# A vision-transformer block on one core: the token-mixing network in five batches, row sums spread over the steps, loads reordered

## What is computed

```python
def _L0_tok_ref(x, w1, b1, w2, b2):
    w = x.sum(axis=1).mean(axis=2)
    h = jax.nn.gelu(w @ w1.T + b1)
    w = h @ w2.T + b2
    w = w.reshape(B, C, G).transpose(2, 0, 1)
    w = jax.nn.softmax(w, axis=0)
    out = jnp.einsum('bgcd,gbc->bcd', x, w)
    return out
...
h = _L0_tok_ref(x, w1, b1, w2, b2)
h = h + attention(layernorm(h))      # 16 heads of 16, causal, 128 tokens an image
h = h + mixture_of_experts(layernorm(h))   # 64 experts, 6 a token, and a shared one
```

## Time and profile before

| stretch, us | what runs | PE | DVE | ACT | POOL | PE clock |
|---|---|---|---|---|---|---|
| 0 to 30 | loads, batch 0 to 3, steps -2 | 8.10 | 14.74 | 7.01 | 4.26 | 1.00 |
| 30 to 75 | steps -1, 0, most of 1 | 33.19 | 17.19 | 27.16 | 2.95 | 0.66 |
| 75 to 240 | steady steps | 158.46 | 145.54 | 132.81 | 94.57 | 1.00 |
| 240 to 300 | loop's end, tables | 45.04 | 41.65 | 15.39 | 33.04 | 0.89 |
| 300 to 510 | expert tiles | 198.07 | 87.07 | 96.41 | 116.06 | 1.00 |
| 510 to 559 | rest of the shared expert, final sums | 29.18 | 33.89 | 2.39 | 1.97 | 0.78 |

### The profile page before, as it was taken

How to read it: one execution, slowest core, us unless ns; L and a number is a source line. 1 busy time by engine, 2 the same in 40 slices (tenths; PEclk the granted TensorE clock), 3 DMA queues, 4 the chain that set the end, 5 groups by cost and what they waited for, 6 DMA issues and landing times. The chain is left out here.

```text
span 559.0 us, 12585 instructions
## 1 busy us (share of the span) xinstructions
PE 472.0 (84%) x2990; PEld 355.2 (64%) x2991; DVE 340.1 (61%) x1054; ACT 281.2 (50%) x910; POOL 252.8 (45%) x277
## 2 busy tenths in 40 slices
PE   0466899999999999987679999999999999997923
PEld 0343676777776766654437787787787787783522
DVE  3715367998999999887753343443443444441797
ACT  2257478877788887871113444444454454441000
POOL 1100111466666666666741546555565565544000
PEclk9967689999999999997899999999999999998967
DMA  8999920011111111121234568557577746542996
GB/s 270 346 333 288 284 60 2 30 67 69 68 59 58 58 66 68 71 75 68 105 110 121 187 190 276 166 170 236 173 211 214 222 143 207 178 150 92 414 360 251
DMA packets 57589, 91.04 MB, mean 163 GB/s; under 512 B 7911, under 2 KB 44650, under 8 KB 57552
## 3 DMA queue, kind: packets, MB, share of 16 engines
q1 hardware_dynamic: 44880, 62.41, 36.9%
q0 software_dynamic: 10368, 26.07, 13.0%
q10 hardware_dynamic: 2304, 2.10, 1.1%
HBM read 87.09 MB, written 41.60 MB: 230 GB/s over the span
## 5 line engine op out<-in xcount | busy, mean ns | idle before, releaser
L392 POOL DMA_INDIRECT y_rows<-y,xring x120 | 118.0, 984 | 108.0 <-issue 67.1
L1021 PE MATMUL ps<-wring,prob 128*128 x480 | 124.5, 382 | 9.1 <-ACT prob L543 9.1
L970 DVE TENSOR_TENSOR probt<-probt,ps 128x128 f32<-128x128 f32 x120 | 34.5, 287 | 119.2 <-ACT probt L548 108.5
L1021 PEld LDWEIGHTS ps<-wring,prob 128*128 128x128 f32 x480 | 81.8, 190 | 17.6 <-issue 11.5
L450 ACT ACTIVATE prob<-ps,nmax 128x128 f32<-128x128 f32 x256 | 69.6, 388 | 5.1 <-DVE nmax L676 3.9
L1021 PE MATMUL ps<-wring,probt 128*128 x240 | 72.0, 382 | 0.0
L548 ACT ACTIVATE probt<-ps 128x128 f32<-128x128 f32 x120 | 33.3, 277 | 71.4 <-PE ps L1021 71.4
L543 ACT COPY prob<-ps 128x256 f32<-128x256 f32 x121 | 45.0, 373 | 47.4 <-PE ps L1236 44.8
L978 DVE TENSOR_SCALAR y<-ps,xring 128x256 f32<-128x256 f32 x120 | 57.8, 483 | 6.4 <-PE ps L1021 4.1
L365 POOL DMA_INDIRECT slot_rows<-row,slot_ix x48 | 52.7, 1097 | 13.7 <-issue 13.4
L365 POOL DMA_INDIRECT slot_rows<-xring,slot_ix x48 | 51.0, 1062 | 14.0 <-issue 14.0
(11 more groups left out here) (177 smaller groups left out, 779.6 us busy)
## 6 DMA issues: line engine op xcount, KB each, us to landing
wring<-wexp SPq DMA_DIRECT2D x121, 384.0 KB
xring<-slot_rows SPq DMA_DIRECT2D x121, 129.0 KB, 2.1
x_sb<-y_rows SPq DMA_DIRECT2D x16, 768.0 KB, 7.3
slot_rows<-pads SPq DMA_DIRECT2D x1, 8256.0 KB, 36.5
x_sb<-x SPq DMA_DIRECT2D x3, 2048.0 KB, 17.8
slot_rows<-pads SPq DMA_DIRECT2D x5, 516.0 KB, 10.3
x_sb<-x SPq DMA_DIRECT2D x4, 512.0 KB, 5.9
out<-h_all ACTq DMA_DIRECT2D x16, 128.0 KB, 6.9
```

The costliest lines, as they stand in the source:

```text
L392: nc.gpsimd.indirect_dma_start(out=y_dram, out_offset=bass.IndirectOffsetOnAxis(ap=xring[:, q, TO_AT:TO_AT + 1].bitcast(I32), axis=0), in_ ...
L970: nc.vector.tensor_tensor(hm[:, q % 2, :], silu[:, q % 2, :], psS[q % 2][:, INTER:2 * INTER], ALU.mult).then_inc(S("h_ready"), 1)
L1021: return nc.tensor.matmul(*a, **k)
```

## The change

The mixing network runs in five batches: image 0, images 1 to 3, then 4 to 7, 8 to 11 and 12 to 15. `part_at` gives each batch its PSUM bank and columns; batches 3 and 4 use columns 64 and up of psC, which the loop also uses. `weights` is split into `shift` and `weights`. Image 0 is mixed, normed and applied ahead of images 1 to 3, whose network runs between (`first_norm`, `first_apply`, and `mixing_in(1)`, `mixing_out(1)` around step -2's turn of image 0); the bias product (`bv_projected`) goes to the end of step -2. Batch 2 keeps the places of the former second batch, in steps 0 and 1. Batches 3 and 4 run in steps 3 and 4, and 7 and 8. ScalarE's row sums, formerly at the top of steps -2, -1 and 0 and inside step 0, stand one or two a step in steps -1 to 6, behind the exponentials of the step. VectorE's sums stand ahead of the loop (image 3) and in step -1 (images 6 and 7). w2 and b2 are loaded ahead of image 1, the constants ahead of image 2.

```diff
--- before.py
+++ after.py
@@ -247,9 +247,16 @@
-        PARTS = ((0, 4), (4, NB))
-        ACT_SUMS = {-3: (0, 2), -2: (4, 5), -1: (6, 7, 8), 0: (9, 10, 12, 14)}
-        DVE_SUMS = {-3: (1, 3), 0: (11, 13, 15)}
+        PARTS = ((0, 1), (1, 4), (4, 8), (8, 12), (12, NB))
+        PART_AT = {0: 2, 3: 3, 7: 4}
+        ACT_SUMS = {-3: (0, 1, 2), -1: (4, 5), 0: (8,), 1: (9,), 2: (10, 11), 3: (12,), 4: (13,), 5: (14,), 6: (15,)}
+        DVE_SUMS = {-3: (3,), -1: (6, 7)}
+        def part_at(part):
+            bank, col = ((psA, 0), (psX, 0), (psC, 0), (psC, E), (psC, E))[part]
+            n = PARTS[part][1] - PARTS[part][0]
+            return bank[0:HID, col:col + n], bank[:, col:col + NG * n]
         TABLES = 4
@@ -279,14 +286,18 @@
         def _(sp):
-            for j in range(4):
+            def load_image(j):
                 sp.dma_start(x_sb[:, j, :, :], x[j].rearrange("g c d -> c g d")).then_inc(x_in[j], 16)
-                if j == 0:
-                    sp.dma_start(w1_sb[:], w1t).then_inc(weights_in["w1"], 16)
-                    sp.dma_start(b1_sb[:], b1).then_inc(weights_in["b1"], 16)
+            load_image(0)
+            sp.dma_start(w1_sb[:], w1t).then_inc(weights_in["w1"], 16)
+            sp.dma_start(b1_sb[:], b1).then_inc(weights_in["b1"], 16)
             sp.dma_start(w2_sb[:], w2t).then_inc(weights_in["w2"], 16)
             sp.dma_start(b2_sb[:], b2).then_inc(weights_in["b2"], 16)
+            load_image(1)
             sp.dma_start(const_sb[:], const).then_inc(const_in, 16)
+            load_image(2)
+            load_image(3)
             sp.dma_start(wqkv_sb[:], wqkv).then_inc(weights_in["wqkv"], 16)
@@ -353,8 +364,9 @@
             pool.wait_ge(S("half_set"), 1)
-            pool.wait_ge(S("var_ready"), 2)
-            roots(0, 2, 1)
+            for n in range(2):
+                pool.wait_ge(S("var_ready"), n + 1)
+                roots(n, n + 1, n + 1)
             pool.wait_ge(S("bias_joined"), 1)
@@ -374,7 +386,7 @@
                     pool.wait_ge(S("var_ready"), b + 4 if b < 0 else 2 * b + 4 if b <= 12 else b + 16)
-                    roots(0 if has(b + 3) else 1, 2 if has(b - 1) else 1, b + 3)
+                    roots(0 if has(b + 3) else 1, 2 if has(b - 1) else 1, b + 4)
                 if has(e):
@@ -420,11 +432,11 @@
-            for img in ACT_SUMS[-3]:
-                sum_image(img)
+            sum_image(0)
             mixing_tanh(0)
+            sum_image(1)
             mixing_exp(0)
-            act.wait_ge(weights_in["bqkv"], 16)
+            sum_image(2)
@@ -435,11 +447,8 @@
                 a, v, cc, d, q = b + 2, b + 1, b - 1, b - 2, 1 - par
-                if isinstance(b, int) and b in ACT_SUMS:
-                    for img in ACT_SUMS[b][0:3 if b else 2]:
-                        sum_image(img)
-                if isinstance(b, int) and b == 1:
-                    mixing_exp(1)
+                if b == 1:
+                    mixing_exp(2)
@@ -483,9 +492,10 @@
                     exp(b, 3)
-                if isinstance(b, int) and b == 0:
-                    for img in ACT_SUMS[0][2:]:
-                        sum_image(img)
+                for img in ACT_SUMS.get(b, ()):
+                    sum_image(img)
+                if b > 1 and b - 1 in PART_AT:
+                    mixing_exp(PART_AT[b - 1])
                 if has(d):
@@ -499,6 +509,9 @@
                         S("xnt_ready"), 1)
+                if b == -2:
+                    mixing_tanh(1)
+                    mixing_exp(1)
                 if has(d):
@@ -522,8 +535,8 @@
                     nc.scalar.copy(ot_sb[:].rearrange("p a k -> p (a k)"), psO[:]).then_inc(S("ot_ready"), 1)
-                if isinstance(b, int) and b == 0:
-                    mixing_tanh(1)
+                if b in PART_AT:
+                    mixing_tanh(PART_AT[b])
                 if isinstance(b, int) and b == NB + 1:
@@ -602,11 +615,11 @@
                 lo, hi = PARTS[part]
-                n, at = hi - lo, psC if part else psA
+                at = part_at(part)[0]
                 dve.wait_ge(weights_in["b1"], 16)
...
                 g = [gel[:, k, lo:hi] for k in range(5)]
-                lk(nc.vector.tensor_scalar(g[0], at[0:HID, 0:n], 1.0 / D, b1_sb[:, 0:1], ALU.mult, ALU.add))
+                lk(nc.vector.tensor_scalar(g[0], at, 1.0 / D, b1_sb[:, 0:1], ALU.mult, ALU.add))
                 lk(nc.vector.tensor_tensor(g[1], g[0], g[0], ALU.mult))
@@ -626,29 +639,33 @@
-            def weights(part):
+            def shift(part):
                 lo, hi = PARTS[part]
-                n, at = hi - lo, psC if part else psA
+                n, at = hi - lo, part_at(part)[1]
                 dve.wait_ge(S("tok_w"), part + 1)
...
                 lk(nc.vector.scalar_tensor_tensor(
-                    out=wtok[:, lo:hi, :], in0=at[:, 0:NG * n].rearrange("p (g b) -> p b g", g=NG), scalar=0.5,
+                    out=wtok[:, lo:hi, :], in0=at.rearrange("p (g b) -> p b g", g=NG), scalar=0.5,
                     in1=b2_sb[:].unsqueeze(1).to_broadcast([P, n, NG]), op0=ALU.mult, op1=ALU.add))
...
                                         ALU.subtract).then_inc(S("tok_shift"), 1)
+            def weights(part):
+                lo, hi = PARTS[part]
+                n = hi - lo
                 dve.wait_ge(S("tok_exp"), part + 1)
...
-            for img in DVE_SUMS[-3]:
-                sum_image(img)
             hidden(0)
             gelu(0)
+            shift(0)
             weights(0)
@@ -801,8 +818,9 @@
                 a, v, cc, d, e, q = b + 3, b + 1, b - 1, b - 2, b - 3, 1 - par
-                if isinstance(b, int) and b == 1:
-                    weights(1)
+                if b == 1:
+                    shift(2)
+                    weights(2)
                     dve.wait_ge(weights_in["gbias"], 16)
@@ -818,6 +836,10 @@
                     place(e, q, 0)
+                    if b in PART_AT:
+                        hidden(PART_AT[b])
+                    if b - 1 in PART_AT:
+                        shift(PART_AT[b - 1])
                 if has(a):
@@ -827,10 +849,11 @@
                         place(e, q, k)
-                if isinstance(b, int) and b == 0:
-                    for img in DVE_SUMS[0]:
+                if b == -1:
+                    for img in DVE_SUMS[-1]:
                         sum_image(img)
-                    hidden(1)
+                if b == 0:
+                    hidden(2)
@@ -872,15 +895,17 @@
                 if has(a):
-                    dve.wait_ge(S("root_ready"), b + 3)
+                    dve.wait_ge(S("root_ready"), b + 4)
                     wait(dve, S("xn_transposed"), a - 1)
...
                 if has(cc):
-                    dve.wait_ge(S("root_ready"), b + 3)
+                    dve.wait_ge(S("root_ready"), b + 4)
                     wait(dve, scattered[cc % NROW], 16 * TOPK * (cc // NROW))
                     apply(image(h_all, cc).unsqueeze(1).to_broadcast([P, TOPK, D]), row_of(cc)[:, :, 0:D], 1).then_inc(S("x2_ready"), 1)
-                if isinstance(b, int) and b == 0:
-                    gelu(1)
+                if b in PART_AT:
+                    gelu(PART_AT[b])
+                if b > 1 and b - 1 in PART_AT:
+                    weights(PART_AT[b - 1])
                 if isinstance(b, int) and b == NB + 1:
@@ -889,26 +914,35 @@
-            dve.wait_ge(weights_in["bqkv"], 16)
-            nc.vector.tensor_scalar(bq_small[:], bqkv_sb[:, 0:2], HD ** -0.5, None, ALU.mult).then_inc(S("qk_bias"), 1)
-            nc.vector.tensor_tensor(bk_half[:], bqkv_sb[:, 2:4].unsqueeze(2).to_broadcast([P, 2, 2]),
-                                    c("half").unsqueeze(1).to_broadcast([P, 2, 2]), ALU.mult).then_inc(S("qk_bias"), 1)
-            nc.vector.tensor_copy(bv_wide[:], bqkv_sb[:, 4:6].unsqueeze(2).to_broadcast([P, KT, P])).then_inc(
-                S("bv_spread"), 1)
-            for n in range(2):
+            def first_norm(n):
                 mix(n, 0)
...
                 nc.vector.bn_stats(st[:, n, :], image(h_all, n)).then_inc(S("ln_chain"), 1)
-            for n in range(2):
-                dve.wait_ge(S("ln_chain"), 2)
+                dve.wait_ge(S("ln_chain"), n + 1)
                 nc.vector.bn_aggr(mv[:, n, :], st[:, n, :]).then_inc(S("var_ready"), 1)
-            dve.wait_ge(S("root_ready"), 1)
-            for n in range(2):
+            def first_apply(n):
+                dve.wait_ge(S("root_ready"), n + 1)
                 apply(image(h_all, n), xn[:, n, :], n).then_inc(S("ln1_done"), 1)
+            first_norm(0)
+            for img in DVE_SUMS[-3]:
+                sum_image(img)
+            first_apply(0)
+            hidden(1)
+            dve.wait_ge(weights_in["bqkv"], 16)
+            nc.vector.tensor_scalar(bq_small[:], bqkv_sb[:, 0:2], HD ** -0.5, None, ALU.mult).then_inc(S("qk_bias"), 1)
+            nc.vector.tensor_tensor(bk_half[:], bqkv_sb[:, 2:4].unsqueeze(2).to_broadcast([P, 2, 2]),
```

(43 more changed lines are left out.)

## The result

The changed kernel takes 555.02 us (median of ten, 553.19 to 557.86) against 560.8 us for the kernel before (median of ten): a ratio of 0.9906, 95% interval 0.988 to 0.9932. The forecast was 555.1.

What follows compares the result with a forecast made beforehand. The start is one chain of waits, with the load of sd at 35.9 us as floor; steady steps are held by TensorE. 560.77 - 13.4 + 7.45 = 554.8 us profiled, 555.1 us as median; range 551 to 560.

Steps and rivals of the forecast that it cites:

- the floor: Top of step 0: load of sd lands at 35.9 us, so step 0 cannot start earlier.
- Step 0: From scores at 35.9 to the second product at 50.1 instead of 63.49; step 1 starts 13.4 us earlier.
- rival (1): Clock falls while TensorE waits for sd; step 0 runs at half clock, 2.65 us more, 557.7 us; chance 0.30.
- What is given back: Steps 1 to 9 lengthen by late row sums and mixing batches, 7.45 us in all.
- Step 2: Two ScalarE sums (2.5 us) against 0.35 us of room lengthen this step by 2.15 us.
- rival (3): Stalls in step 2 and around step 4's mixing products each drop the clock, 4 us each; 565.8 us; chance 0.08.
- Step 3's 0.6: Step 3: one ScalarE sum of 1.25 us, with a TensorE wait for bank psC beside it, costs 0.6 us.
- The room of 0.65: Steady step: ScalarE's copy x2t ends 0.65 us before TensorE's gate matmul needs it, so each sum costs 0.6.
- Step 8: The last batch's mixing_out, 1.84 us at low clock, taken as half at full clock, adds 0.95 us.
- (2): Late sums hide in ScalarE's idle time; only mixing work, 2.9 us, is given back; 550.5 us; chance 0.07.
- (4): Constants' load holds image 0 at 10 to 12 instead of 9; step 0 at most 2 later; 556-557 us; chance 0.08.
- (5): Splitting costs in full: two batches in series and unhidden cost 6.5 us instead of 2.9; 558.7 us; chance 0.06.

Runs made afterwards that it cites:

- old-order runs: Changed kernel with loads in the former order: 606.39 us, ratio 1.0018; also with gate, sgu and sd waits moved to steps 2 and 16: 603.20 us, 0.9975.
- no-floor run: Changed kernel with TensorE's wait for gate moved from step 0 to step 2, for sgu and sd to step 16; 599.58 us, ratio 0.9889.
- doubled-sums run: Changed kernel plus a second, unused ScalarE pass before row sums in steps 3-6; 607.45 us (ratio 0.9967) on chip 6, 589.49 us (0.9914) on chip 4.
- idle-sums run: Changed kernel with row sums of images 8 to 15 moved into idle time of VectorE and ScalarE in steps 0 and 1; 598.56 us, ratio 0.9871.

## Why the prediction was right

**Image 0 and step -1.** First product 5.6 forecast, 5.49 measured; constants 9.0, 8.47; gelu 10.0, 10.38; projections 21.35 and 32.35, 21.55 and 31.64; the floor at 35.9, 35.92. The chain held row by row. Two errors cancelled in it: the constants came 0.5 us earlier than taken, and the casts behind them took 1.9 us (8.47 to 10.38) instead of 0.95. The old-order runs show the size of the early loads (2.6 to 2.8 us at the end of step 0, without the floor) and the no-floor run that of the floor (2.6 with the fall of the clock behind it, 1.0 to 1.2 without). Image 1's projection came 0.7 us before its forecast, and the floor swallowed that. No run undid the splitting of the first batch or put ScalarE's early sums back, so the share of each in the 12.84 us is read from the timelines and not shown apart.

**Step 0.** The forecast put the product at 50.1 and it came at 50.65. That looks like a miss of 0.55 us and is two of opposite sign. The forecast's own sizes were 1.0 us too long: with the clock up, as in the doubled-sums run, the product comes 13.1 us after the start of step 0, at 49.1. ScalarE's stretch from the turned probabilities to the next image's exponentials took 5.8 us there (38.27 to 44.10), where the forecast had 6.8 (38.2 to 45.0). And the clock fell behind the 2.23 us stall, as rival (1) says, late and for 3.4 us, which cost 1.4 to 1.6 us. Where it fell fully, in the idle-sums run, the price was 2.9 us, near the rival's 2.65. So rival (1) was not an alternative to the forecast but a matter of degree from one profile to the next: no fall, one and a half microseconds, or 2.9. That the sum without it came so near is luck.

**What is given back.** 7.45 forecast, 8.51 measured. Steps 1, 4, 5, 6, 7 and 9 are within 0.11 us. For step 1 that hangs on the clock: at the same 7 us of low clock the step takes 12.5 us without a sum (four profiles) and 13.4 with one (two), so the sum costs 0.9 there and not 0.6, and 3 us more of low clock cost a further 1.1. Step 2 failed in its second part: the stall of two sums was right (2.15 forecast, 1.97 measured without a fall, 1.91 idle), but the sum had no term for the clock behind it. It stood as rival (3), with 0.08 and 4 us a fall; it happened in six of seven profiles, at 1.4 to 2.1 us in step 2. The chance was far too low, because one row, the stretch at 246 to 248, was taken for a rule; the price was too high. Its upper bound, half speed held from before 26.28 to behind 39.05, was not one stretch: the granted clock of the kernel before is 1.00 from 30 to 32 us and falls at 32 (0.58 from 32 to 34). Step 3's 0.6 was wrong the other way: a sum is free there (12.93 with it, 12.94 to 12.97 without), and what was measured is the mixing's 0.2. The room of 0.65 was read from one steady step. Step 8 is 0.5 above its term, and its cause was not tried apart.

**The rivals.** (2), hidden sums, falls for step 2 by the idle-sums runs and holds for step 3. (4) falls, the constants came early. (5), the splitting's own cost in full, would be 3.25 us a batch, where the forecast had 1.95 for the last one (steps 7 to 9): it costs 1.4 us on chip 4 and 2.4 in the table, nearer to the forecast than to (5) on both.

**The total.** 554.8 was forecast for the profiled execution, and that took 557.86, 3.1 us more. By step 10 it had gained 4.33 us where the forecast had 5.95 (0.55 less gained at the start, 1.06 more given back), and 1.4 of the 4.33 were lost behind it. That the median of ten comes within 0.1 us of the forecast owes something to chance. And the gain of 1% is that of one chip: on chip 13 it was 0.2%, inside the noise, and on chip 4 the kernel with the doubled sums, which does more work, was 0.9% below the kernel before.

## What to carry to other kernels

Work that an engine can do at any time belongs where that engine is idle in the profile, not spread evenly: the sums of images 9 to 11, with the fall of the clock behind them, cost 5.0 us in steps 1 and 2, where the next reader was half a microsecond away, and all of the late sums together cost nothing that can be seen where both engines waited anyway. Before shortening a start, look for waits that stand earlier than their use; one wait moved to the first reader was worth 2.6 us at the end of step 0, as much as the new order of the loads. And where TensorE is made to stand for about two microseconds in a dense stretch, put the clock's fall behind it into the sum, at its chance and price, and not into a rival: of the thirteen stalls of 1.87 to 2.98 us that these profiles have at the top of step 0 and in step 2, ten were followed by one.

## What the runs showed of the hardware

The same idle of 1.91 us in the same place was followed by a fall of the granted clock to 0.50 in six profiles and left it at 1.00 in one. At the top of step 0 the clock stayed up behind 1.87 and 1.92 us, fell for 3.4 us behind 1.94, 2.23 and 2.42, and for 6.8 behind 2.98. Behind the 3.10 to 3.13 us at the end of step 0 it fell in all twelve profiles of changed kernels, for 7 to 10 us. It also fell once, at 34 us in the old-order run without the floor, where the longest idle of TensorE in the 6 us before had been 1.30 us.

The granted clock of both profiles on the first chip reads 1.00 up to 32 us, but the 16 matmuls of a projection took 3.78 us at 21.55 and 2.05 at 31.64. So the value of 1.00 for 0 to 30 us in the table of the kernel before is not to be trusted, and the durations are.

VectorE's cast of 128x128 values took 1.28 us beside GpSimd's memset of 1290 columns, where it took 0.21 before, beside GpSimd's copy, which in its turn fell from 1.13 to 0.26 us (both engines, first 11 us of the changed kernel):

```profile
8.47 1.28 DVE L628 CAST ident_b<-const_sb 128x128 bf16<-128x128 f32 x1 [1.89 <-DMA const_sb<-const]
8.50 1.17 POOL L354 MEMSET pads<- 128x1290 f32 x1 [8.09 <-DMA const_sb<-const]
8.62 1.60 DVE L630 CAST causal_b<-const_sb 128x128 bf16<-128x128 f32 x4
...
10.38 0.14 DVE L639 SCALAR_TENSOR_TENSOR gel<-gel 32x1 f32<-32x1 f32 x1
```

It was the same, 1.28 us, in all twelve profiles of changed kernels. What in the two engines collides was not tried apart.

Three chips of four took 6 to 8% longer for the same kernel. On them ScalarE waits before its copies in most steps from about step 4 on, for up to 3.2 us, with the releaser outside the core, and nothing in the trace explains it. What it is stays open.
